# Two transformer layers on one core: where LayerNorm is applied, where the LoRA term and the first attention maxima stand among the products, and how one layer's query and key blocks travel

## The reference, cut to what matters

```python
x = x + 0.5 * dora(LN(x))              # FFN_A
x = x + attn0(LN(x))                   # QKV0, attention, WO0
x = x + 0.5 * dora(LN(x))              # FFN_B
x = x + 0.5 * moe(LN(x))               # MOE_A
x = x + attn1(LN(x))                   # QKV1, attention, WO1
x = x + 0.5 * moe(LN(x))               # MOE_B
```

## Time and profile before

| | |
|---|---|
| median of 3 runs | 1398.65 us (1390.51 to 1400.39) |
| the profiled execution's own time | 1391.04 us |
| its span, first to last instruction | 1389.3 us |
| mean granted clock of TensorE | 0.923 of full speed (2.4 GHz) |
| busy: PE, PEld | 1220.1 us (88%), 753.2 us (54%) |
| busy: DVE, ACT, POOL | 1017.3 us (73%), 573.0 us (41%), 412.5 us (30%) |
| DMA | 76.19 MB, mean 55 GB/s |

### The profile page before, as it was taken

One profiled execution on the slowest core, in us unless ns is written; L12 is line 12 of the kernel. 1 busy time (PEld: TensorE's weight loads), 2 busy tenths in 40 slices (PEclk: granted clock), 3 DMA queues, 4 the chain that ended last, 5 costly groups with the idle time before them and its releaser, 6 DMA issues.

```text
span 1389.3 us, 21472 instructions
## 1 busy us (share of the span) xinstructions
PE 1220.1 (88%) x6800; PEld 753.2 (54%) x6800; DVE 1017.3 (73%) x2894; ACT 573.0 (41%) x827; POOL 412.5 (30%) x601
## 2 busy tenths in 40 slices
PE   3888999999898878997868989999988987889877
PEld 1675444443377765444756744444435776744367
DVE  5778899997168967744858888999852798686266
ACT  1221576665622252553212126666655223435421
POOL 1531231121265400216415413122214562002262
PEclk9996699998899997999989958999999999979999
DMA  8346211220010022000040742112200100120001
GB/s 308 114 129 152 93 42 32 55 63 2 1 48 1 1 46 70 1 2 25 37 169 0 207 110 81 25 25 55 63 2 1 48 0 16 31 70 2 1 9 54
DMA packets 37283, 76.19 MB, mean 55 GB/s; under 512 B 5084, under 2 KB 6620, under 8 KB 37036
## 3 DMA queue, kind: packets, MB, share of 16 engines
q1 hardware_dynamic: 37176, 74.82, 18.6%
HBM read 48.98 MB, written 27.08 MB: 55 GB/s over the span
## 4 chain that ended last, share of the span: by engine, by line
PE 62%; DVE 25%; issue 5%; ACT 4%; DMA 2%; SPq 1%; POOL 1%; DVEq 0%; ACTq 0%; POOLq 0%
PE bank L986 16%; PE bank L860 12%; PE bank L768 5%; PE bank L970 4%; DVE maxes L1208 4%; PE bank L770 4%; PE bank L769 4%; PE bank L964 3%; PE bank L754 3%; DVE probs L1044 3%; DVE unused L1204 2%; DVE ops L1147 2%; PE bank L870 2%; DVE stats L1029 2%; DVE gate L1089 2%
## 5 line engine op out<-in xcount | busy, mean ns | idle before, releaser
L1407 ACT ACTIVATE probs<-bank 128x1024 f32<-128x1024 f32 (+3 forms) x416 | 368.1, 911 | 333.1 <-PE bank L970 226.2
L860 PE MATMUL bank<-ops 48*128 48x512 f32 (+3 forms) x960 | 320.0, 439 | 22.8 <-DVE maxes L1204 8.1
L1204 DVE CUSTOM_DVE_ANT_0 unused<-bank,causal 128x128 bf16<-128x128 f32 (+3 forms) x640 | 279.6, 485 | 39.6 <-PE bank L860 36.0
L1522 POOL TENSOR_SCALAR_AFFINE_SELECT probs<-probs 128x256 f32<-128x256 f32 (+1 forms) x256 | 118.8, 464 | 635.3 <-ACT probs L1407 635.1
L860 PEld LDWEIGHTS bank<-ops 48*128 48x128 f32 (+1 forms) x960 | 162.8, 207 | 205.7 <-DVE maxes L1204 84.1
L986 PE MATMUL bank<-probs,v_mem 128*17 128x512 f32 (+6 forms) x1920 | 255.5, 524 | 6.1 <-ACT heads_raw L1394 5.6
L1208 DVE TENSOR_REDUCE maxes<-bank 128x1 f32<-128x512 f32 x320 | 207.0, 683 | 41.0 <-PE bank L860 39.6
L970 PE MATMUL bank<-ops 50*128 50x512 f32 (+2 forms) x640 | 176.7, 452 | 9.1 <-DMA ops<-shiftT 4.8
L1315 ACT CAST xT<-bank 128x512 fp32r<-128x512 f32 (+1 forms) x96 | 52.5, 551 | 232.0 <-PE bank L754 232.0
L768 PE MATMUL bank<-ops,xT 128*128 128x512 f32 (+1 forms) x288 | 116.4, 404 | 24.6 <-DVE x L1064 19.0
L970 PEld LDWEIGHTS bank<-ops 50*128 50x128 f32 x640 | 87.5, 199 | 66.3 <-issue 34.7
(11 more groups left out here) (114 smaller groups left out, 2012.3 us busy)
## 6 DMA issues: line engine op xcount, KB each, us to landing
query_rows_dram<-ops SPq DMA_DIRECT2D x48, 256.0 KB, 3.5
ops<-query_rows_dram SPq DMA_DIRECT2D x64, 192.0 KB, 4.2
w_odd<-staging_wqkv SPq DMA_DIRECT2D x4, 1536.0 KB, 6.7
x<-x_dram SPq DMA_DIRECT2D x16, 256.0 KB, 6.0
ops<-ops SPq DMA_DIRECT2D x16, 256.0 KB, 3.0
out_dram<-x SPq DMA_DIRECT2D x16, 256.0 KB, 2.0
staging_wqkv<-wqkv_dram SPq DMA_DIRECT2D x2, 1536.0 KB, 16.1
key_rows_dram<-ops SPq DMA_DIRECT2D x24, 128.0 KB
```

What stands on the lines that cost most here:

```text
L860: last = mm(dst[:, h * w:(h + 1) * w], queries(a, u)[rows, t // 4, hi, t % 4 * P:(t % 4 + 1) * P], keys(a, u, hi)[rows, HALF * kp:HALF * k ...
L1204: V.tensor_tensor_reduce(unused[:, masked % 3, 0:w], part, causal[:, HALF - w:], 1.0, NEG, ALU.add, ALU.max, dst).then_inc(s["max_done"].s ...
L1407: A.activation(probs[:, e % 6, :, 0:cols], scores[:, 2 * (e % 2):2 * (e % 2) + 2, 0:cols], ACT.Exp, scale=a.scale).then_inc(s["exp"].sem, 1)
L1522: G.affine_select(out=p, in_=p, compare_op=ALU.is_ge, fill=0.0, base=0, pattern=pattern, channel_multiplier=-1).then_inc(s["masked"].sem, 1)
```

## The change

- LayerNorm: the statistics are taken three ticks ahead; VectorE also computes variance plus epsilon and minus the mean (two 128x1 operations). ScalarE multiplies mean and rstd and normalises with one Identity activation, two ticks ahead, into one of six buffers.
- MoE: TensorE turns the weighted rows of the product before ahead of the first half and adds its LoRA product after the first half's second chunk. VectorE's order becomes: low part, epilogue of the product one tick ago, statistics, routing, weighing. The expert numbers 0 to 7 are read from PSUM, where ScalarE copies them once in each WO stage.
- QKV0: its tiles are turned a tick later; the second four value products come before blocks (3, 0) to (4, 1); maxima stand between the chunks of the last four blocks, and all 28 of `ring_first` are done there.
- QKV1: one ScalarE and one VectorE operation per block on 128 rows, into four buffers in `features`; three stores to DRAM rows per block, and loads of 96 rows per head back. 14 maxima stand between chunks.

```diff
-            order = [(0, 0), (1, 0), (2, 0), first, (0, 1), (1, 1), (2, 1), (3, 0), (4, 0), (3, 1), (4, 1), second]
-            self.begun = {8: 3, 9: 6, 10: 9, 11: 12}
+            order = [(0, 0), (1, 0), (2, 0), first, (0, 1), (1, 1), (2, 1), second, (3, 0), (4, 0), (3, 1), (4, 1)]
+            self.ring_in = {8: (1, 1, 2, 2), 9: (1, 1, 2, 2), 10: (2, 2, 2, 2), 11: (2, 2, 2, 2)}
         else:
             order = [(0, 0), (1, 0), first, (3, 0), (0, 1), (1, 1), (3, 1), second, (2, 1), (2, 0)]
-            self.begun = {5: 2, 6: 4, 7: 6, 8: 9, 9: 12}
+            self.ring_in = {5: (0, 0, 1, 1), 6: (1, 1, 1, 1), 8: (0, 0, 1, 1), 9: (1, 1, 2, 2)}
...
-        early = len(plain) - (3 if chain[-2] in MOE_RANK else 4)
+        early = len(plain) - 3
...
+            def standard_operands(b):
                 a, s = A1, qs[QKV1]
...
+                for n, (j, g) in enumerate(blocks1):
+                    rows = (k1_rows if j % 2 else q1_rows)[4 * (j // 2):4 * (j // 2) + 4].rearrange(
+                        "h (p d) s -> p h d s", p=3)[:, :, :, HALF * g:HALF * (g + 1)]
+                    hi, lo = (m.bitcast(F32) for m in high_low(n))
+                    sp.wait_ge(s["hi"].sem, s["hi"].at(b, n + 1))
+                    sp.dma_start(rows[0], hi).then_inc(block_stored[n].sem, 16)
+                    sp.dma_start(rows[1 if j % 2 else 2], hi).then_inc(block_stored[n].sem, 16)
+                    sp.wait_ge(s["read"].sem, s["read"].at(b, a.product_no("qk", j, g) + 1))
+                    sp.dma_start(rows[2 if j % 2 else 1], lo).then_inc(block_stored[n].sem, 16)
+                    if n % 2 == 1:
+                        load_standard(b, n - 1)
+                        load_standard(b, n)
+
+            def load_standard(b, n):
+                j, g = blocks1[n]
+                half = slice(HALF * g, HALF * (g + 1))
+                sp.wait_ge(block_stored[n].sem, block_stored[n].at(b, 48))
...
-                copy_high(b)
+                standard_operands(b)
...
+                        for _ in range(in_chunk[chunk[0] - 1]):
+                            ring_item(b, att, ring_no[0])
+                            ring_no[0] += 1
+                    if before is not None:
+                        turn_hw(b, *before)
                     if tick.product is not None and tick.product[0] in MOE_RANK:
-                        expert_half(b, *tick.product, True)
-                        if before is not None:
-                            turn_hw(b, *before)
-                        expert_half(b, *tick.product, False, between=lora_between)
+                        expert_half(b, *tick.product, True, between=lora_between)
+                        expert_half(b, *tick.product, False)
...
+                dve.wait_ge(ln_mv.sem, ln_mv.at(b, n + 1))
+                V.tensor_scalar(var_eps[:, n % STAT_SLOTS, :], mv[:, n % STAT_SLOTS, 1:2], EPS, None, ALU.add
+                                ).then_inc(ln_eps.sem, 1)
+                V.tensor_scalar(minus_mean[:, n % STAT_SLOTS, :], mv[:, n % STAT_SLOTS, 0:1], -1.0, None, ALU.mult
+                                ).then_inc(ln_minus.sem, 1)
...
-                V.tensor_scalar(gate[:, 1, :], expert_no[:], top_atf[:, 1:2], route[:, 0:1], ALU.is_equal, ALU.mult
+                V.tensor_scalar(gate[:, 1, :], numbers, top_atf[:, 1:2], route[:, 0:1], ALU.is_equal, ALU.mult
...
-                    for h in range(4):
-                        hi, lo = head_rows1(j, h, g)
-                        last = V.scalar_tensor_tensor(lo, src[32 * h:32 * (h + 1), :], bias_head1[:, 4 * j + h:4 * j + h + 1],
-                                                      hi.bitcast(F32), ALU.add, ALU.subtract)
-                    last.then_inc(s["read"].sem, 1)
+                    n = blocks1.index((j, g))
+                    hi, lo = high_low(n)
+                    dve.wait_ge(s["hi"].sem, s["hi"].at(b, n + 1))
+                    V.scalar_tensor_tensor(lo, src, bias_qk1[:, j:j + 1], hi.bitcast(F32), ALU.add, ALU.subtract
+                                           ).then_inc(s["read"].sem, 1)
...
                     for it in tick.turns:
                         turned_lo(b, *it)
-                    for it in ticks[i + 2].turns if i + 2 < len(ticks) else ():
+                    if before is not None:
+                        epilogue(b, *before)
+                    for it in ticks[i + 3].turns if i + 3 < len(ticks) else ():
                         statistics(b, *it)
...
+                A.mul(ln_bias[:, i, :], minus_mean[:, i, :], rstd[:, i, :]).then_inc(ln_scaled.sem, 1)
+                act.wait_ge(ln_scaled.sem, ln_scaled.at(b, n + 1))
...
+                A.activation(xn[n % XN_SLOTS], x[:, t, :], ACT.Identity, bias=ln_bias[:, i, :], scale=rstd[:, i, :]
+                             ).then_inc(xn_ready.sem, 1)
```

More of the change, by code:

```diff
@@ L360, in carve @@
             return work[:, at[0] - n:at[0]]
-        xn = [carve(D) for _ in range(2)]
+        xn = [carve(D) for _ in range(XN_SLOTS)]
         cos_t = carve(SEQ)
@@ L394, in rope_set, with high_low @@
             return prods, hi, lo
+        def high_low(n):
+            return (features[:, 1024 * (n % 4) + HALF * i:1024 * (n % 4) + HALF * (i + 1)].bitcast(F32R) for i in range(2))
         def queries(a, u):
@@ L416, in build @@
         qkv_banks = [bank[:, 6, :], bank[:, 3, :], bank[:, 2, :]]
+        numbers = bank[:, 7, 2 * P:2 * P + EXPERTS]
         hw_turns = [bank[:, 7, 0:P], bank[:, 7, P:2 * P]]
@@ L884, in operands_ready @@
                 else:
[L885 to L888 removed]
+                    for g in range(1 + (t >= 4 or u > 0)):
+                        pe.wait_ge(std_keys[u // 2, g].sem, std_keys[u // 2, g].at(b, 16))
+                        pe.wait_ge(std_queries[u, g].sem, std_queries[u, g].at(b, 16))
             def ring_free(b, st, i):
@@ L1161, in chain @@
                 first_heads = len(ticks) - (len(ATT[att].ticks) if att else 0)
-                for i in range(len(ticks) + 1):
-                    tick = ticks[i] if i < len(ticks) else Tick()
+                ring_no = 0
+                for i, tick in enumerate(ticks):
                     experts = tick.product is not None and tick.product[0] in MOE_RANK
-                    before = [ticks[i - n].product if 0 <= i - n < len(ticks) else None for n in (1, 2)]
-                    if before[1] is not None and before[1][0] in MOE_RANK:
-                        epilogue(b, *before[1])
-                    if before[0] is not None and before[0][0] not in MOE_RANK:
-                        epilogue(b, *before[0])
+                    before = ticks[i - 1].product if i else None
                     for it in tick.turns:
                         turned_lo(b, *it)
-                    for it in ticks[i + 2].turns if i + 2 < len(ticks) else ():
+                    if before is not None:
+                        epilogue(b, *before)
+                    for it in ticks[i + 3].turns if i + 3 < len(ticks) else ():
                         statistics(b, *it)
@@ L1364, in chain @@
                         copy_turned(b, st, t)
+                        if t == 0 and st in WO_ATT:
+                            A.copy(numbers, expert_no[:]).then_inc(numbers_ready.sem, 1)
                         nb, nst = (b, st + 1) if st < MOE_B else (b + 1, FFN_A)
@@ L1370, in chain @@
                         copy_hw(b, *before.product)
+                    for it in ticks[i + 2].turns if i + 2 < len(ticks) else ():
+                        normalise(b, *it)
                     if tick.product is not None and tick.product[0] in MOE_RANK:
@@ L1479, in chain @@
                 ticks, att = TICKS[c], ATT_OF_CHAIN.get(c)
-                for tick in ticks[0:2]:
+                for tick in ticks[0:3]:
                     for it in tick.turns:
@@ L1492, in chain @@
                         bias_x(b, st, t)
-                    if att == QKV0 and i:
-                        for p in ticks[i - 1].heads:
-                            if p[1:] in ropes:
-                                n = ropes.index(p[1:])
-                                if n < 4:
-                                    rope_low(b, n)
-                                else:
-                                    rope_sums(pool, G, b, n)
+                    if att == QKV0:
+                        for p in ticks[i - 1].heads if i else ():
+                            if p[1:] in ropes[:4]:
+                                rope_low(b, ropes.index(p[1:]))
+                        for p in tick.heads:
+                            if p[1:] in ropes[4:]:
+                                rope_sums(pool, G, b, ropes.index(p[1:]))
             def attention(b, st):
```

150 lines of the change are left out of this document (69 added, 81 removed).

## The result

The kernel after takes 1458.79 us in the median of 4 runs (1454.64 to 1460.46), the kernel before 1396.16 us on the same chip: a ratio of 1.0447 with a 95% interval of 1.040 to 1.0494. It is 4.5% slower, where 1360 us was forecast. The profiled execution took 1454.64 us with a span of 1452.9 us, 63.6 us above the span of before; the mean granted clock is 0.897.

The account below looks back on a forecast made before the run. The last-ending chain was 62% TensorE and 25% VectorE, with TensorE idle 50.1 us for VectorE's normalising. Terms summed to -36.0 us from 1391.04, giving 1355, plus 5 for the median: 1360 us, likeliest range 1345 to 1375.

Parts of the forecast that it names:

- FFN_A: Feed-forward stage: normalising two ticks ahead on ScalarE takes VectorE's tick off TensorE's path; -5.5 us in each sequence.
- C2: From the attention's end through WO1, MOE_B and the next sequence's FFN_A to its next block: -5.5, -8.0 and -2.7 us.
- Expert tiles and WO1: New expert loop: MOE_A -6.5 us each, MOE_B -8.0 and -2.7; WO1, through two ticks of lead, -2.7 each.
- C1: From the attention's end through WO0, FFN_B and MOE_A to the next block; the claim was MOE_A's -6.5 us.
- C3: WO1 and MOE_B after the last attention: -2.7 us for each of the two.
- rival 2: Expert stages: hold-ups stay, caused by the pointer scalar or GpSimd's share; +21 us, 1381 us; chance 0.10.
- Rotated blocks: QKV0 to first scores: later last product, then a 13.9 us tail to the shift rows; +5.8 and +7.7 us.
- VectorE ends at 54.7: QKV0: VectorE's 21.5 us from the first maximum, with 3 us lost at the 13th, end 54.7 us after the start.
- Standard blocks: QKV1 to first scores: whole-block operations save more than stores and loads cost; 59 us against 63.7, -4.7 each.
- stores to 44.8, landed 47.7: QKV1, after the last product at 42 us: final stores issued until 44.8 and landed by 47.7 us.
- rival 3: DMA queue delays all four first scores: standard +11 us each, rotated +9 each, half clock +4 each; 1407 us; chance 0.12.
- Rivals 1, 2 and 4: 1: rotated blocks cost nothing, 1346 us (0.22); 2: gate hold-ups stay, 1381 (0.10); 4: GpSimd holds up small operations, 1391 (0.03).

Follow-up runs that it names:

- the version put together: Kernel after with 128-row standard stores, the rotated order of before, and unit 0's shift rows ahead of bulk loads: 1325.25 us, 0.9489 of before.

## Why the prediction was wrong, step by step

- **FFN_A, forecast -5.5 us:** -7.2 at the start; the mechanism holds in its half on the lead (VectorE normalising two ticks ahead keeps all but 1 us of it), the size is 1.7 us more. The second one lies in C2.
- **Expert tiles and WO1:** C1 forecast -6.5, measured -6.2 and -6.6; C2 -5.5 - 8.0 - 2.7 = -16.2, measured -18.4; C3 -5.4, measured -4.2. MOE_A's ticks of 6.75 and 5.82 us were forecast as 6.7 and 5.6. The sums were right, the reason only in part: I put the gain on the new loop and took the short gates as its side effect, and rival 2 priced the hold-ups at 21 us. The runs show them worth some 32 us in the kernel before and 42 in this one; the new loop with the gates still in SBUF is slower than the old (C1 121.0 for 111.9).
- **Rotated blocks, forecast +5.8 and +7.7:** measured +9.8 and +16.7. The first maxima, the 3 us at the 13th (2.2 and 2.7 us in the trace) and the tail of 13.9 us (14.0: last product at 117.4, scores at 131.4) came as written. What failed is the step "VectorE ends at 54.7", and with it the last product "at about 51.0": its 21.5 us of work from the first maximum on came out at 22.2 busy, but with 6 us of waits for TensorE in 28.3 us, where the forecast had 3, and 10 us of them in 32 in the second sequence, in part at the half clock. The last product ended 54.5 and 58.5 us after the start. VectorE was not the bound of that stretch alone. The tail I counted as given; that rows ready at 107.7 us needn't stand in it, I had not seen.
- **Standard blocks, forecast -4.7 each:** measured +39.4 and +37.5, and this is most of the miss: 86 us of the 99 between 1360 and 1459. The failed step is "stores to 44.8, landed 47.7", and before it "issued to 28, landed 31": the stores were priced as issues of 0.6 us, from four rotated stores in the earlier trace rows, and their bytes only within "some 190 GB/s" of the loads. The rotated stores have 16 heads outermost, these have 4, and so a block's three stores took some 7.7 us (768 KB at 102 GB/s, an estimate) instead of the forecast's 3 from issue to landing. SyncE, in order, then stood before the next block's stores too. TensorE's wait for the keys (0,1), forecast at 3 us, was 24.97; the last product ended 78.2 and 75.5 us after the start instead of 42, and the tail to the first scores was 24.6 and 25.3 us instead of 17. With 128 rows outermost the stage is 63.0 and 65.7 us: there the tail is 17.0 and 17.6, as forecast, and the wait for the keys is 5.4 and 6.4, so that the last product ends at 46.0 and 48.1. The 4 to 6 us over the forecast's 59 lie there.

```profile
526.10 0.77 PE L882 MATMUL bank<-ops 96*128 96x512 f32 x1 [5.40 <-DMA ops<-standard_key_rows_dram]
```

- **The rivals:** rival 3 had the place (standard blocks late through transfers) and the sign, but its 1407 us rest on stores of 1.2 us, where a store of 256 KB at 100 GB/s takes 2.6: +11 us in a standard stage instead of +38. It had a chance of 0.12. Like the forecast it has no room for a store that runs on a quarter of the engines. Rivals 1, 2 and 4 didn't occur: first scores came later than before, gates stayed at 0.28 us, and the small operations at 0.14 to 0.16.

## What to carry to other kernels

Before a DMA pattern is priced from another one's row, compare the outermost dimension, not the bytes: a store with 4 there ran on a quarter of the engines, and cutting it by hand cost SyncE twelve issues a block where another layout kept three (its loads, cut in three, went from 12 to 36 a sequence). When work is moved earlier, look in each in-order queue for what it frees and is still behind something bulky: here 23 us lay in one line's place. And an operation that meets another engine's at the same point of every tick can cost that one's whole length; put its operand elsewhere, or move it.

## What had not been expected of the hardware

What a store moves: about 100 GB/s for 256 KB stores with 4 rows outermost, 350 to 450 GB/s with 128. An operation of 128x8 elements on VectorE took up to 1.7 us beside GpSimd's 1.8 us in the kernel with the numbers in SBUF, and 0.28 in all 32 cases with its operand in PSUM. TensorE's granted clock was 0.61 and 0.50 over the first 20 us of standard attentions that began some 12 us sooner in their stage, and these attentions took 6 and 12 us longer; 5.0 and 4.6 us of that are the wait for shift rows, the rest went with the clock. What sets it there was not isolated, only that in the version put together, without that wait, the same 20 us ran at 0.80 and 0.77 and the attentions took 87.4 and 89.4 us. The late LoRA was not tried alone.
